# Attention and MoE block on one core: softmax halves by column chunk, merged loads, LoRA pieces between the steps, four expert pairs in whole fp32

## The chip, the cores and the metric

The kernel runs on one core of a Trainium2 chip. The metric is device time in microseconds (us). A core has a matrix engine (TensorE, PE; its weight loads are shown apart as PEld), VectorE (DVE), ScalarE (ACT), GpSimd (POOL), and a sync engine (SP) that here issues most of the transfers from memory. The engines run their own instruction lists in order and meet at semaphores.

## The reference, cut

One layer over 128 tokens (4 batches of 32, width 256), all in fp32: a causal cross-attention, a self-attention whose four projections carry a rank-16 LoRA update, and a mixture of 32 experts with 4 chosen for each token, each behind a layer norm and added to the residual stream.

```
x = x + xattn(layernorm(x), ctx, Wq, Wkv, Wout)          # 16 heads of 16, causal, ctx has 64 columns
x = x + attn(layernorm(x), W + 0.5 * A @ B for q, k, v, o)  # with biases
h = layernorm(x)
s = sqrt(softplus(h @ router.T)); pick top 4 of s + bias; p = s / sum(s)
x = x + sum_e p_e * ffn_e(h) + ffn_shared(h)
ffn(h) = (silu(clip(h @ wg.T)) * clip(h @ wu.T)) @ wd.T  # clip at +-7, inner width 128
```

## The kernel before

All 128 tokens fill the 128 partitions, and nothing is looped but heads, chunks and experts. Width 256 is two chunks c of 128. The residual stream is kept in PSUM twice: `bY` (tokens on partitions) and `bXT` (transposed). The work is one dependent sequence, in three stages.

**Cross-attention** (a = 0). TensorE centres x (L390 to L391), projects keys from the context (L395) and queries (`project_T`, L323), and computes `values` (L332) ahead of `scores` (L344, L348). VectorE spreads the keys over heads (`spread_keys`, L713), takes the row maximum and subtracts it (`shift_half`, L722, L724). ScalarE copies the values into `v_heads` (`copy_v`, L578), then does the exponentials (`exp_half`, L570). TensorE transposes the probabilities (L357) and multiplies them by the values (`attend`, L365); VectorE divides (`normalise_heads`, L752, L754); TensorE transposes (L372), ScalarE copies (L608), and the output projection is added to `bY` (L376) and `bXT` (L380). A half of a softmax is one value of g, that is, of the 64-row group of the keys; each half writes both column chunks. In the original the columns of the output weights are permuted to fit this (`order`).

**Self-attention** (a = 1). The norm takes its statistics from `bY` (L780), GpSimd raises the variance to -0.5 (L282), TensorE spreads it (L441), and VectorE writes the normed `xnT` (L791). Keys, queries, values and the same softmax follow. The projections' weights had the LoRA update merged before: eight small matmuls (`merge_lora` of TensorE, L316, in two blocks of four, two of which run at the same time in different rows of the array) and VectorE's additions (`merge_lora`, L744, and L784 with `wo_mean`, L788). ScalarE's `woc` (L629) is the centred output weight.

**Mixture of experts.** The 32 experts go as 16 pairs. Gate and up weights of a pair (512 KB) are loaded to `gu_raw` (8 buffers). They aren't multiplied as fp32: ScalarE rounds them to fp32r (`gu_high`, L591), GpSimd subtracts to get the rest (`gu_low`, L291, two instructions a pair), the activations are split in the same way (L638, L640, L810), and TensorE makes three products for each of two chunks (`gate_up_half`, L500), six matmuls of 512 columns a pair. TensorE starts on pairs 1 to 5 while VectorE, ScalarE and GpSimd work out the router (L836 to L869: a chain of small operations, some 30 columns wide, each waiting for the one before). Then, for each pair: `clip` (L827), `silu_unit` (L667), `gate_h` (L880), `transpose_h` (L516), `hT_unit` (L672), `down` (L525), with `gate_up(n + 4)` between. GpSimd runs through `gu_low` without regard to the router. `keep_warm` (L309) puts idle-time matmuls of 512 columns at ten places.

The sync queue issues eleven loads (L236), then gate-and-up loads (`load_gu`, L242), of which those from the ninth on wait for `gu_lo_ready` (their buffer), and down loads (`load_dn`, L245). The last step copies `bY` out (L894).

## Time and profile before

| | before |
|---|---|
| time, median of 3 runs (lowest to highest) | 82.14 us (82.06 to 82.21) |
| the profiled execution | 81.89 us |
| its span, first to last instruction | 79.8 us |
| PE, PEld, DVE, ACT, POOL busy | 71.0, 54.8, 46.6, 42.8, 43.5 us |
| mean granted TensorE clock | 0.976 |

The profiled execution stands 0.25 us below the median, and 2.1 us of it lie outside its span. Positions below are microseconds from the start of the span. Busy time of TensorE includes the idle-time matmuls. A matmul on fp32 operands shows as two records, one on fp32r or bf16 operands as one, and a transpose as one.

### The profile page before, as it was taken

What the parts mean: (1) busy time and instruction counts of PE and PEld (TensorE: products, weight loads), DVE (VectorE), ACT (ScalarE), POOL (GpSimd) and SP (SyncE); (2) the same over time, 40 slices, a digit from 0 to 9 for tenths busy, and PEclk for the clock granted to TensorE, in tenths of its full rate; (3) what the DMA queues carried; (4) which work ended last, traced back from release to release, by engine and by line L of the source; (5) the groups of instructions that cost most, each with busy time, mean ns of one, the idle gap of its engine ahead of it and who ended that gap; (6) DMA issues with size and microseconds to landing.
All of it is one profiled execution on the core that took longest, in us unless ns stands there. A gap on an engine that the chain in (4) does not pass through costs nothing.

```text
span 79.8 us, 1534 instructions
## 1 busy us (share of the span) xinstructions
PE 71.0 (89%) x557; PEld 54.8 (69%) x557; DVE 46.6 (58%) x118; ACT 42.8 (54%) x90; POOL 43.5 (54%) x49
## 2 busy tenths in 40 slices
PE   2999999696989999999618999999999999999960
PEld 1388675484966676887306788887888878888840
DVE  2028675377775706999999854566444664449320
ACT  1513951929359288406916986668866633336400
POOL 7200200549999216990830799999999994000000
PEclk9999999999999999999995699999999999999999
DMA  1998999999999999279718209970000000000001
GB/s 27 319 242 237 383 417 402 410 409 412 398 391 405 388 402 390 101 187 306 304 18 273 103 8 267 375 267 3 0 0 0 0 8 0 0 0 0 0 0 66
DMA packets 6440, 15.80 MB, mean 198 GB/s; under 512 B 737, under 2 KB 1634, under 8 KB 6434
## 3 DMA queue, kind: packets, MB, share of 16 engines
q1 hardware_dynamic: 6210, 15.49, 54.5%
q10 hardware_dynamic: 224, 0.23, 1.0%
q8 instruction: 4, 0.07, 0.3%
q14 instruction: 2, 0.02, 0.1%
HBM read 15.59 MB, written 0.13 MB: 197 GB/s over the span
## 4 chain that ended last, share of the span: by engine, by line
PE 57%; DVE 16%; DMA 9%; SPq 6%; issue 3%; ACT 3%; POOL 1%
PE bY L525 17%; DMA gu_raw<-moe_w_dram 9%; SPq L236 6%; PE bB L500 6%; PE bXT L516 5%; PE bC L500 4%; PE bA L500 4%; PE bE L500 4%; PE bD L500 4%; PE bY L376 2%; PE bXT L467 2%; PE bA L332 2%; DVE gu_clip L827 2%; PE bY L550 2%; DVE key L862 1%
## 5 line engine op out<-in xcount | busy, mean ns | idle before, releaser
L291 POOL TENSOR_TENSOR gu_w<-gu_raw,gu_w 128x512 fp32r<-128x512 f32 x32 | 39.9, 1288 | 15.7 <-ACT gu_w L591 15.7
L591 ACT ACTIVATE gu_w<-gu_raw 128x1024 fp32r<-128x1024 f32 x16 | 16.7, 1050 | 1.6 <-DMA gu_raw<-moe_w_dram 1.6
L525 PE MATMUL bY<-dn_w,hT 128*128 128x256 f32 x64 | 16.3, 380 | 0.0
L672 ACT ACTIVATE hT<-bXT 128x256 f32<-128x256 f32 (+1 forms) x17 | 6.4, 377 | 14.4 <-PE bXT L516 14.4
L525 PEld LDWEIGHTS bY<-dn_w,hT 128*128 128x128 f32 x64 | 11.0, 190 | 0.9
L516 PE MATMUL bXT<-first_sb,h 128*128 128x128 f32 x33 | 6.7, 282 | 2.4 <-DVE h L880 2.4
L516 PEld LDWEIGHTS bXT<-first_sb,h 128*128 128x128 f32 x33 | 4.8, 145 | 5.1 <-DVE h L880 2.8
L500 PE MATMUL bB<-gu_w,xnT_parts 128*128 128x512 f32 x24 | 7.9, 461 | 0.1
L500 PEld LDWEIGHTS bB<-gu_w,xnT_parts 128*128 128x128 f32 x24 | 5.0, 218 | 1.5 <-DVE xnT_parts L810 0.5
L282 POOL TENSOR_TENSOR rstd<-var_eps,inv_sqrt_power 128x1 f32<-128x1 f32 x3 | 1.7, 554 | 6.9 <-DVE var_eps L698 5.3
L500 PE MATMUL bC<-gu_w,xnT_parts 128*128 128x512 f32 x18 | 5.3, 428 | 0.0
L500 PE MATMUL bE<-gu_w,xnT_parts 128*128 128x512 f32 x18 | 5.1, 417 | 0.0
L500 PE MATMUL bA<-gu_w,xnT_parts 128*128 128x512 f32 x18 | 5.1, 417 | 0.0
L500 PE MATMUL bD<-gu_w,xnT_parts 128*128 128x512 f32 x18 | 5.1, 416 | 0.0
L309 PE MATMUL bE<-warm_sb 128*128 128x512 bf16 x7 | 3.1, 559 | 1.4 <-DVE warm_sb L759 1.4
L880 DVE SCALAR_TENSOR_TENSOR h<-gu_clip,gate,bB 128x128 f32<-128x128 f32 x8 | 2.4, 345 | 2.6 <-ACT bB L667 2.6
L500 PEld LDWEIGHTS bE<-gu_w,xnT_parts 128*128 128x128 f32 x18 | 3.4, 188 | 0.7
L500 PEld LDWEIGHTS bA<-gu_w,xnT_parts 128*128 128x128 f32 x18 | 3.4, 188 | 0.7
L500 PEld LDWEIGHTS bD<-gu_w,xnT_parts 128*128 128x128 f32 x18 | 3.4, 188 | 0.7
L500 PEld LDWEIGHTS bC<-gu_w,xnT_parts 128*128 128x128 f32 x18 | 3.4, 189 | 0.7
L880 DVE SCALAR_TENSOR_TENSOR h<-gu_clip,gate,bE 128x128 f32<-128x128 f32 x6 | 1.8, 345 | 3.1 <-ACT bE L667 3.1
L880 DVE SCALAR_TENSOR_TENSOR h<-gu_clip,gate,bD 128x128 f32<-128x128 f32 x6 | 1.8, 344 | 2.5 <-ACT bD L667 2.5
(208 smaller groups left out, 130.1 us busy)
## 6 DMA issues: line engine op xcount, KB each, us to landing
gu_raw<-moe_w_dram SPq DMA_DIRECT2D x16, 512.0 KB, 8.3
dn_w<-moe_w_dram SPq DMA_DIRECT2D x16, 256.0 KB, 6.3
aw_sb<-attn_w_dram SPq DMA_DIRECT2D x2, 512.0 KB, 6.5
shared_sb<-shared_w_dram SPq DMA_DIRECT2D x1, 384.0 KB, 10.1
xwq_sb<-x_wq_dram SPq DMA_DIRECT2D x1, 256.0 KB, 3.4
lora_sb<-lora_dram SPq DMA_DIRECT2D x1, 256.0 KB, 4.1
xwo_sb<-x_wo_dram SPq DMA_DIRECT2D x1, 256.0 KB, 6.2
first_sb<-first_dram ACTq DMA_DIRECT2D x1, 130.0 KB, 2.8
```

The lines of the kernel that those rows point to most:

```text
L236: sp.dma_start(dst, src).then_inc(ld[name], 16)
L282: nc.gpsimd.tensor_tensor(rstd[:, n:n + 1], var_eps[:, n:n + 1], inv_sqrt_power[:], ALU.pow).then_inc(rstd_ready, 1)
L291: nc.gpsimd.tensor_tensor(gu_w[:, p % SLOTS, 1, cols], gu_raw[:, p % RAW, cols], gu_w[:, p % SLOTS, 0, cols], ALU.subtract).then_inc(gu_lo ...
L309: nc.tensor.matmul(bank[:, :], warm_sb[:, 0:128], warm_sb[:, :], start=True, stop=True)
L332: last = nc.tensor.matmul(bank[j * S:(j + 1) * S, b * NG * HD:(b + 1) * NG * HD], x_t(k)[:, b * S:(b + 1) * S], w(k).rearrange("p (n j d) ...
L376: return nc.tensor.matmul(bY[:, 0:D], heads_outT[:, a, g, :], w[:, g, :], start=False, stop=(g == DC - 1), skip_group_check=True)
L500: last = nc.tensor.matmul(bGU[n % 5][:, 0:GU], xnT_parts[:, a, k, :], gu_w[:, (n - 1) % SLOTS, w, k * GU:(k + 1) * GU], start=(k == 0 and ...
L516: last = nc.tensor.transpose(bHT[n % 2][:, e * T:(e + 1) * T], h[:, n % 2, e, :], ident)
L525: last = nc.tensor.matmul(bY[:, 0:D], hT[:, n % 2, e, :], dn_w[:, at:at + D], start=False, stop=(n == PAIRS and e == 1), skip_group_check= ...
L591: nc.scalar.activation(gu_w[:, p % SLOTS, 0], gu_raw[:, p % RAW], ACT.Copy).then_inc(gu_hi_ready, 1)
L672: nc.scalar.activation(hT[:, n % 2, 0:width], bHT[n % 2][:, 0:width * T], ACT.Copy).then_inc(hT_ready, 1)
L880: last = nc.vector.scalar_tensor_tensor(h[:, n % 2, e], gu_clip[:, n % 4, e, 1, :], weight_e, bank[:, e * 2 * I:e * 2 * I + I], ALU.mult, ...
```

## The change

What it does, part by part:

1. **Halves by column chunk.** In both softmaxes a half is now one chunk c, with the two row groups g in two banks side by side (`bP[c]`, a tile of two banks). Scores of half c need queries and keys of chunk c alone, and the score matmuls alternate between row groups. Each of the 8 score matmuls of a half now raises `scores_ready`. Output weights need no permuting.
2. **Order of the cross-attention.** The values come behind the scores; their copies are shared between ScalarE (j = 0, 1) and VectorE (j = 2, 3), and the copy of the transposed probabilities as well. The variance of the first norm no longer comes from VectorE's statistics: ScalarE squares the centred x, and two one-column matmuls sum it.
3. **Loads.** x transposed, identity, centring matrix and head mask are one load (`head`, 264 KB), x and the causal mask one (`x_mask`), context and both key and value weights one (`ctx_kv`), the cross-attention's output weights part of `small`. The sync queue issues seven loads before the experts' instead of eleven; ScalarE's queue two, as before.
4. **LoRA pieces.** Each of the eight small matmuls stands alone or in twos at a place where TensorE waits, and VectorE merges them in seven additions. `keep_warm` stays at the start (6) and behind the keys (1). `wo_mean` is ScalarE's.
5. **Four whole pairs.** Pairs 0 to 3 are multiplied as fp32 straight from `gu_raw` (two matmuls of 512 columns, K = 128, a pair). ScalarE and GpSimd convert only pairs 4 to 15. ScalarE does two conversions before the router (pairs 4, 5) where it did six.
6. **GpSimd waits.** Behind pairs 4 and 5 it waits for the third norm and then for `gate_ready`, the end of the router.
7. **Load conditions.** The loads come in the order 4, 5, 6, 0, shared, 1, 2, 3, 7; pairs 8 to 11 wait for `gu_lo_ready` of pairs 4 to 7, pairs 12 to 15 for `gu_ready` of pairs 0 to 3.

The diff, cut to its core:

```diff
@@ constants and tiles
-WARM = dict(start=5, keys=1, heads0=1, headsT0=1, rstd=2, norm=2, probs1=2, attend1=2, heads1=1, headsT1=1)
+WARM = dict(start=6, keys=1)
+WHOLE = 4
+def raw_slot(p):
+    return p if p < RAW else (p - WHOLE) % RAW
@@ sync
+            for name, dst, src in (("head", head_sb[:], head), ("xwq", xwq_sb[:], x_wq), ("lora", lora_sb[:], lora),
+                                   ("aw_kq", aw_sb[:, 0:2], attn_w[:, 0:2]), ("small", small_sb[:], small),
+                                   ("aw_vo", aw_sb[:, 2:4], attn_w[:, 2:4]), ("rows", rows_sb[:], rows)):
             def load_gu(p):
-                if p >= RAW:
+                if p >= RAW + WHOLE:
+                    sp.wait_ge(gu_ready, p - RAW - WHOLE + 2)
+                elif p >= RAW:
                     for c in range(DC):
                         sp.wait_ge(gu_lo_ready[c], p - RAW + 1)
@@ gpsimd
             inverse_sqrt(0)
+            inverse_sqrt(1)
...
-            for p in range(PAIRS):
+            for p in range(WHOLE, PAIRS):
                 for c in range(DC):
-                    if (p, c) == (0, 1):
-                        inverse_sqrt(1)
-                    if (p, c) == (4, 1):
+                    if (p, c) == (WHOLE + 2, 0):
                         inverse_sqrt(2)
+                        pool.wait_ge(gate_ready, 1)
                     gu_low(p, c)
@@ tensor
+            def scores(a, c):
+                for g in range(2):
+                    r = slice(64 * g, 64 * g + 64)
+                    if a == 0:
+                        nc.tensor.matmul(bP[c][:, g, 0:128], causal_sb[:, 0:128], causal_sb[:, 128:],
+                                         start=True, stop=False, skip_group_check=True)
+                for b in range(B):
+                    for g in range(2):
+                        r = slice(64 * g, 64 * g + 64)
+                        nc.tensor.matmul(bP[c][b * S:(b + 1) * S, g, 0:G * S], qT[r, a, c, b * S:(b + 1) * S],
+                                         k_heads[r, c, :, b * S:(b + 1) * S],
+                                         start=(a == 1), stop=True, skip_group_check=True).then_inc(scores_ready, 1)
...
+            for c in range(DC):
+                pe.wait_ge(q_ready, c + 1)
+                pe.wait_ge(k_ready, c + 1)
+                scores(0, c)
+            values(bE, lambda k: ctx_sb[L:2 * L, 0:T], lambda k: ctx_sb[L:2 * L, T:T + D], 1, range(B))
...
+            transpose_probs(0, 1)
+            merge_lora(0, 0)
+            pe.wait_ge(probsT_dve_ready, 1)
+            pe.wait_ge(v_act_ready, 1)
+            pe.wait_ge(v_dve_ready, 1)
             attend(0, 0)
+            merge_lora(0, 1)
+            pe.wait_ge(probsT_act_ready, 1)
             attend(0, 1)
+            merge_lora(1, 0)
+            merge_lora(3, 0)
+            transpose_heads(0, 0)
+            merge_lora(1, 1)
+            merge_lora(2, 0)
+            transpose_heads(0, 1)
...
+            def gate_up_whole(n, k):
+                return nc.tensor.matmul(bGU[n % 5][:, 0:GU], xfT[:, k, :], gu_raw[:, raw_slot(n - 1), k * GU:(k + 1) * GU],
+                                        start=(k == 0), stop=(k == DC - 1))
...
-            for n in range(2, 6):
+            for n in range(2, WHOLE + 1):
                 gate_up(n)
+            pe.wait_ge(xt_lo_ready, 1)
+            gate_up(WHOLE + 1)
             transpose_h(0, width=1)
+            transpose_h(1)
@@ scalar
-            copy_v(range(G), range(B), bV[0]).then_inc(v_act_ready, 1)
-            exp_half(0, 0)
-            exp_half(0, 1)
-            copy_probsT(0)
-            copy_probsT(1)
-            gu_high(0)
+            exp_half(0, 0)
+            copy_v(0, range(B), bE[:, 0:D])
+            exp_half(0, 1)
+            copy_v(1, range(B), bE[:, 0:D]).then_inc(v_act_ready, 1)
+            nc.scalar.activation(probsT[:, 1], bP[1][:, 0, 0:DC * T], ACT.Copy).then_inc(probsT_act_ready, 1)
             for c in range(DC):
                 act.wait_ge(headsT_psum, c + 1)
...
+            gu_high(WHOLE)
...
-            gu_high(2)
-            gu_high(3)
+            gu_high(WHOLE + 1)
...
-            gu_high(5)
...
-            gu_high(6)
             nc.scalar.preload_act_table(ACT.Silu)
+            gu_high(WHOLE + 2)
             silu_unit(0)
             silu_unit(1)
+            gu_high(WHOLE + 3)
@@ vector
             shift_half(0, 0)
             shift_half(0, 1)
+            copy_probsT(0, 0)
+            copy_v(2, range(B), bE[:, 0:D])
+            copy_v(3, range(B), bE[:, 0:D]).then_inc(v_dve_ready, 1)
             dve.wait_ge(ld["aw_kq"], 16)
-            merge_lora(0)
-            merge_lora(1)
+            merge_lora(0, 0)
             normalise_heads(0, 0)
             normalise_heads(0, 1)
+            merge_lora(0, 1)
+            merge_lora_whole(1)
...
-            nc.vector.tensor_scalar(wo_mean[:], wo_sum[:], -1.0 / D, None, ALU.mult).then_inc(wo_mean_ready, 1)
```

## Rows read from the trace of the kernel before

**Rows 1.** The profile's page: busy time by engine; the chain's shares.

```profile
PE 71.0 (89%) x557; PEld 54.8 (69%) x557; DVE 46.6 (58%) x118; ACT 42.8 (54%) x90; POOL 43.5 (54%) x49
...
PE 57%; DVE 16%; DMA 9%; SPq 6%; issue 3%; ACT 3%; POOL 1%
```

**Rows 2.** Windows A:B in us: busy (records) by engine, clock, DMA share, GB/s.

```profile
39.20:41.60 2.40, 0.02 (x2) 0.02 (x1) 2.23 (x10) 0.96 (x3) 1.48 (x2) 1.00 0.13 49
42.40:44.00 1.60, 1.60 (x5) 1.31 (x6) 1.60 (x5) 1.20 (x2) 0.00 (x0) 0.50 0.87 328
```

**Rows 3.** The chain in order of time, experts' stage: start, us, what.

```profile
43.93 2.10 PE bB L500 x6
...
47.11 1.41 PE bC L500 x6
48.52 0.22 PE bXT L516 x2
48.74 0.87 PE bY L525 x4
...
77.27 0.42 DVE y_sb L894
```

**Rows 4.** Timeline of VectorE in the router: start, us, operation.

```profile
32.10 1.30 DVE L836 SCALAR_TENSOR_TENSOR clip_at<-var_eps,rstd 128x1 f32<-128x1 f32 x2 [0.66 <-POOL rstd L282]
...
33.59 1.00 DVE L842 TENSOR_SCALAR den<-one_plus 128x32 f32<-128x32 f32 x1
...
35.01 0.83 DVE L844 TENSOR_TENSOR den<-den,e_abs 128x32 f32<-128x32 f32 x1
...
35.88 0.19 DVE L846 SCALAR_TENSOR_TENSOR ratio<-ln_one_plus,den 128x32 f32<-128x32 f32 x1
...
38.35 1.16 DVE L862 SCALAR_TENSOR_TENSOR key<-score,small_sb 128x32 f32<-128x32 f32 x1
...
40.07 0.67 DVE L866 SCALAR_TENSOR_TENSOR weight<-replaced,score 128x33 f32<-128x33 f32 x1
```

**Rows 5.** Timeline, other engines around the router.

```profile
31.45 0.53 PE L536 MATMUL bXT<-small_sb,xfT 128*128 128x32 f32 x4
...
38.11 1.28 ACT L660 ACT_TABLE_LOAD   x1
...
44.34 16.22 POOL L291 TENSOR_TENSOR gu_w<-gu_raw,gu_w 128x512 fp32r<-128x512 f32 x13 [3.65 <-ACT gu_w L591]
```

**Rows 6.** Timeline of the two attentions, steps that mark the stages.

```profile
7.01 0.65 PE L332 MATMUL bE<-wv_sb,ctx_sb 64*32 64x64 f32 x32
...
8.52 0.42 DVE L722 TENSOR_REDUCE row_max<-bA 128x8 f32<-128x256 f32 x1 [0.73 <-PE bA L348]
...
9.17 0.48 PE L316 MATMUL bD<-lora_sb 16*128 16x256 f32 x1
...
9.17 0.48 PE L316 MATMUL bC<-lora_sb 16*128 16x256 f32 x1
...
12.25 0.21 DVE L752 RECIPROCAL inv_sum<-bE 128x8 f32<-128x8 f32 x1 [0.52 <-PE bE L365]
...
13.83 1.06 ACT L591 ACTIVATE gu_w<-gu_raw 128x1024 fp32r<-128x1024 f32 x1 [1.60 <-DMA gu_raw<-moe_w_dram]
...
16.34 0.43 DVE L780 BATCH_NORM_STATS2 stats<-bY 128x6 f32<-128x256 f32 x1 [1.71 <-PE bY L376]
...
17.89 1.18 DVE L788 TENSOR_SCALAR wo_mean<-wo_sum 128x2 f32<-128x2 f32 x1
...
18.98 0.41 DVE L791 TENSOR_TENSOR xnT<-xcT,bA 128x256 f32<-128x256 f32 x1
```

**Rows 7.** Timeline, VectorE's step that ends the attentions.

```profile
30.10 0.29 DVE L814 COPY xfT<-bXT 128x128 f32<-128x128 f32 x1 [2.36 <-PE bXT L380]
```

**Rows 8.** The chain in order of time, one of its idle-time matmul pairs.

```profile
25.24 0.43 PE bB L309 x2
```

**Rows 9.** The view of the tile gu_raw: issue to landing of its 16 loads.

```profile
DMA to landing us min/median/max: 3.7/8.3/13.3
```

More of the change, by code:

```diff
@@ L178, in build @@
         q_ready = sem("q_ready")
[L179 removed]
+        lora_psum = [sem(f"lora_psum_{m}") for m in "kqvo"]
         lora_merged = sem("lora_merged")
@@ L509, in gate_up @@
                 for k in range(DC):
-                    last = gate_up_half(n, k)
+                    if n <= WHOLE:
+                        pe.wait_ge(ld_gu[n - 1], 16)
+                        last = gate_up_whole(n, k)
+                    else:
+                        pe.wait_ge(gu_lo_ready[k], n - WHOLE)
+                        for a, w in HI_LO:
+                            last = nc.tensor.matmul(bGU[n % 5][:, 0:GU], xnT_parts[:, a, k, :],
+                                                    gu_w[:, (n - 1) % SLOTS, w, k * GU:(k + 1) * GU],
+                                                    start=(k == 0 and a == w == 0), stop=(k == DC - 1 and a == 1))
                 last.then_inc(gu_ready, 1)
@@ new lines @@
+    head[:, XT:XT + DC * T] = x.T.reshape(DC, 128, T).transpose(1, 0, 2).reshape(128, -1)
+    head[:, IDENT:IDENT + 128] = np.eye(128, dtype=np.float32)
+    head[:, CENTRE:CENTRE + 128] = np.eye(128, dtype=np.float32) - np.float32(1.0 / D)
+    head[:, HMASK:HMASK + G] = np.arange(128)[:, None] // HD % G == np.arange(G)[None, :]
+    causal = np.zeros((128, 128 + G * S), np.float32)
+    causal[:, 0:128] = np.eye(128)
+    hidden = np.arange(S)[None, :] > (np.arange(T) % S)[:, None]
+    causal[:, 128:] = np.tile(np.where(hidden, -1e30, 0.0), (1, G))
@@ L950 @@
     moe = np.concatenate([gu, dn], axis=2).reshape(128, -1)
-    arrays = {"x": x, "x_t": x.T.reshape(DC, 128, T).transpose(1, 0, 2), "first": first, "small": small,
-              "causal": causal, "ctx_k": ctx_k, "w_v": w_kv[D:].T,
-              "x_wq": chunked(v["L0_xattn_Wq"]), "x_wo": chunked(v["L0_xattn_Wout"][:, order]), "lora": lora,
-              "rows": rows, "attn_w": attn_w, "shared_w": shared, "moe_w": moe}
+    arrays = {"head": head, "x_mask": x_mask, "small": small, "ctx_kv": ctx_kv, "x_wq": chunked(v["L0_xattn_Wq"]),
+              "lora": lora, "rows": rows, "attn_w": attn_w, "shared_w": shared, "moe_w": moe}
     arrays = {n: np.ascontiguousarray(a) for n, a in arrays.items()}
```

556 lines of the change are left out of this document (252 added, 304 removed).

## The prediction

> **What bounds the kernel now.** I read the page's busy times and the chain's shares first [rows 1]: TensorE is busy 89% of the span but carries 57% of the chain, so for a good part of the time somebody else decides. The chain in order of time then shows three stages. From 46 us to the end it is TensorE alone, with a period of 1.41 + 0.22 + 0.87 = 2.50 us a pair [rows 3]. From 30 to 42 us it is the router on VectorE [rows 4]; TensorE has pairs 1 to 5 to do meanwhile, runs out at 39.2 and stands 2.4 us, after which its granted clock falls to half [rows 2]. The first product behind takes 2.10 us where it otherwise takes 1.41 [rows 3]. Before 30 us the chain changes engines at every step, and I followed it by the steps that mark the stages [rows 6, 7].
>
> **Start of the span to the statistics of the first residual (16.34, [rows 6]).** The row maximum of half one starts at 8.52. In front of the scores the values (0.65) go away; I count the context's load, issued 0.4 earlier, as 0.25 for keys and queries; two one-column products for the variance come in, four records behind the queries, at the price of the logits' four (0.45 by their spacing, [rows 5]); eight score products alternate between row groups, where two products at once in two row groups are seen for LoRA (both at 9.17, [rows 6]), minus 0.35. Sum -0.65 - 0.25 + 0.45 - 0.35 = -0.8, so 7.7. From there to the first reciprocal I keep the 3.7 us (12.25 becomes 11.4): the values' copies are now behind the scores, but shared between two engines. From the reciprocal to the statistics it took 4.1 us. In it ScalarE waited for a load until 13.83 and converted to 14.89 before it could copy the heads [rows 6]. That conversion is now behind the copies. New sum from 11.4: first division 0.5, second half attended and divided to 12.6, one LoRA couple ahead of each heads' transpose (0.43 each, a 256-column product alone being 0.87/2, [rows 3]) to 13.1, copy to 13.5, two products to 14.2. That is 2.8 instead of 4.1, and -2.1 in all.
>
> **To the normed x (18.98).** VectorE had `wo_mean` in front of it: 1.18 us for two numbers a partition, while GpSimd was converting [rows 6]. It moves to ScalarE; of its 1.18 us some 0.7 lay beside the wait for GpSimd's power and the spreading product, so it frees 0.5 to 0.9. Against it LoRA piece (3, 1), 0.43, stands ahead of that spreading product, about 0.3 of it on the path. Net -0.5: xnT at 16.4, in all -2.6.
>
> **To the end of the attentions (30.10, [rows 7]).** 11.1 us before. The chain holds idle-time matmuls twice 0.43 and once 0.22 [rows 8]; they go. Scores of half one wait for chunk 0 only, a gain of some 0.4. What comes in: `woc` (two ScalarE steps) and a values' copy now stand ahead of the exponentials (I take +0.2), a LoRA merge ahead of the row maximum (0.42, +0.3), the values' second half between the two transposes (0.65, in place of the fillers there). Net -1.05: xfT at 26.45, in all -3.65. LoRA in six places takes 2.6 us of TensorE where two blocks took 1.7; except for the 0.3 and the couples above, it lies in waits. If none did, it would cost 6 x 0.43 = 2.6; if all, I gain 0.7 more.
>
> **The router and the first pairs.** Taking positions as before (all less 3.65 at the end): TensorE starts on the whole pairs at 30.5. A whole pair is two fp32 products of 512 columns; 256 columns cost 0.43, so 1.73 a pair against 1.41 [rows 3]: dearer by 0.32. Its work is 4 x 1.73 + 1.41 (pair five) + 0.45 (logits) + 0.87 (shared) = 9.6, to 40.1. The router's small steps with both inputs in SBUF took 1.30 (for two), 1.00, 0.83, 1.16 and 0.67 where GpSimd had an instruction running, and 0.19 for the same width at 35.88 where it had none [rows 4]. With GpSimd waiting I take 0.4, 0.2, 0.2, 0.2, 0.25: -3.7, of which 0.7 is lost because `den` waits for ScalarE's sum. So `gate`, ready at 41.3, comes at 38.3. ScalarE has the table load (1.28, [rows 5]), one conversion (1.06, [rows 6]) and two silus ahead of the first gated pair: h(1) at 39.3. TensorE is still at work until 40.1, a cover of 0.8 us: its idle 2.4 us and the slow clock go together. Transposes, a wait of 0.3 for hT and the shared down product end at 41.2; the next pair at full clock at 42.6, where it ended at 46.03. So -3.4 here.
>
> **The rest** keeps 2.50 us a pair if conversions keep up. GpSimd made 13 in 16.22 us, 2.50 a pair [rows 5]: exactly TensorE's pace, so what lead it has at the start it keeps. It begins pair 6 at 38.3, done 40.8, wanted at 43.7 + 0.7: a lead of 3.6. The load of pair 10 now waits on the sync queue for `gu_low` of pair 6, and pairs 11 to 15 and their down loads are queued behind it. Issued at 40.8 it lands 3.7 to 13.3 later, median 8.3 with the engines full [rows 9]. The queue is empty at that point, so I take 3.7: 44.5, wanted by ScalarE at 45.0. The first loads come in fewer, wider pieces; the very first, 264 KB, may land 0.3 earlier or 0.5 later than two of half the size did.
>
> **Sum.** 79.8 - 3.65 - 3.4 = 72.75 us of span, + 2.1 outside = 74.85 against the profiled 81.89; the median of the runs stands 0.25 above that execution: **75.1 us**.
>
> Each of 8 score products now raises a semaphore. The Trainium skill ("TensorE: Matmul & The Clock Gate", The cost: per-tile semaphore tail) fits 26.3 ns for each further increment. By that rule, as an estimate, a half ends 0.18 us later, four halves at most 0.7, and the sum would be 75.3 to 75.8. No row of this trace shows such a row of increments.
>
> **The rivals.**
> (a) *The clock falls in the attentions*, since the idle-time matmuls go. For: the clock did fall after TensorE stood [rows 2]. Against: that was 2.4 us, and the longest gap in my new order is some 0.6. Price as at the router: 2.10 - 1.41, and about 1.0 on the products just ahead, 1.7: 76.8. Chance 0.14.
> (b) *Conversions or their loads set the pace.* For: equal pace, and pair 10's load is held until 40.8. If it lands after 8.3, ScalarE stands 4.1 us with hT behind it; slack there is 1.3: +2.8, 77.9. Against: empty queue. Chance 0.1.
> (c) *The router's stalls aren't GpSimd's.* Then h(1) stays near 42, TensorE stands 2 us and the clock falls: only about 1.1 of the 3.4 stays, 77.4. Against: the 0.19 row. Chance 0.04.
> (d) *Slower than before: the clock stays low from the attentions into the pairs.* Without fillers TensorE enters the experts' stage at half clock, whose 9.6 us of products then double: 75.1 + 9.6 = 84.7. It decides from 7 us of products done at half clock on the path. For: before, the products behind the stand ran at half clock although they were packed [rows 2]. Against: from 47.11 on they are at full speed again, some 5 us after the stand [rows 3], and my order has no such stand. Chance 0.03.
> (e) *The first stages don't shrink as summed*: waits that I took for hidden are on the path, half of 3.65 is gone, 76.9. Chance 0.12. The forecast itself, 73.7 to 76.5, keeps 0.57.
>
> **How the numbers follow.** The lower end takes all covers as full: LoRA hidden (0.7) and 0.8 more for `wo_mean` and the load, 73.6. The upper end takes in (a), (c), (e) and most of (b): 77.9. About 0.2% is what a measurement of this kernel tells from no change; all cases but (d) are faster by more: 0.96 faster, 0.01 the same, 0.03 slower.
>
> **What would show it.** Router steps of 0.2 us with GpSimd idle; no gap of TensorE between the pairs and the first transpose, and a granted clock of 1.0 from 40 us on; xnT near 16.4 and xfT near 26.5; first output statistics near 14.2; a period of 2.50 to the end; GpSimd's last conversion some 3 us before it is wanted. Wrong would be: a gap of TensorE before the heads' transposes, ScalarE waiting for `gu_raw` of pair 10, a clock under 1.0 between 5 and 30.

## The result, and the profile after

| | before | after |
|---|---|---|
| median (lowest to highest), same chip | 82.17 us (82.06 to 84.07) | 79.49 us (79.29 to 80.41) |
| ratio after/before, 95% interval | | 0.970 (0.960 to 0.980) |
| profiled execution, its span | 81.89, 79.8 us | 79.66, 77.9 us |

Ratios rest on the executions that agree with each other; where too few did, only the times are given. The change makes the kernel faster by 2.7 us where I had forecast 7.0, outside my range. The page of the changed kernel, busy times and shares of the chain, against [rows 1]:

```profile
PE 72.9 (94%) x544; PEld 53.4 (69%) x544; DVE 42.7 (55%) x119; ACT 38.0 (49%) x84; POOL 33.7 (43%) x42
...
PE 85%; DMA 5%; ACT 3%; DVE 3%; issue 1%
```

VectorE's 16% of the chain are 3% now. TensorE carries 85% of it, 57% before: that is the first sign of what I missed, since in that kernel little that TensorE does is free.

**The router and the pairs.** The timeline of VectorE after, against [rows 4], and GpSimd's first six conversions behind the router, against [rows 5]:

```profile
33.56 0.23 DVE L848 SCALAR_TENSOR_TENSOR clip_at<-var_eps,rstd 128x1 f32<-128x1 f32 x2 [0.44 <-POOL rstd L293]
...
34.47 0.18 DVE L854 TENSOR_SCALAR den<-one_plus 128x32 f32<-128x32 f32 x1 [0.34 <-ACT one_plus L669]
...
35.07 0.19 DVE L856 TENSOR_TENSOR den<-den,e_abs 128x32 f32<-128x32 f32 x1
...
37.76 0.19 DVE L874 SCALAR_TENSOR_TENSOR key<-score,small_sb 128x32 f32<-128x32 f32 x1
...
38.51 0.20 DVE L878 SCALAR_TENSOR_TENSOR weight<-replaced,score 128x33 f32<-128x33 f32 x1
...
38.95 0.30 DVE L881 TENSOR_SCALAR gate<-weight,weight_sum,rstd 128x32 f32<-128x32 f32 x1
...
39.33 7.51 POOL L304 TENSOR_TENSOR gu_w<-gu_raw,gu_w 128x512 fp32r<-128x512 f32 x6 [5.80 <-DVE gate L881]
```

Each step that took 0.67 to 1.30 us takes 0.18 to 0.23. `gate` is ready 7.8 us after xfT, where it took 11.2. Two windows of the changed kernel (columns as in [rows 2]), and the chain behind them (against [rows 3]):

```profile
36.00:40.00 4.00, 4.00 (x11) 1.77 (x10) 3.60 (x17) 3.71 (x7) 0.67 (x1) 1.00 0.01 2
40.00:44.00 4.00, 3.85 (x19) 2.93 (x18) 3.13 (x8) 2.93 (x7) 4.00 (x4) 1.00 0.27 51
```

```profile
42.67 1.40 PE bP L529 x6
44.08 0.22 PE bXT L537 x2
44.29 0.87 PE bY L546 x4
```

The stand of 2.4 us and the fall of the clock to half are gone, and the period is 2.50 as before.

**The front.** The marks of the stages on VectorE after, against [rows 6] and [rows 7]:

```profile
10.65 0.43 DVE L737 TENSOR_REDUCE row_max<-bP 128x8 f32<-128x256 f32 x1 [0.61 <-PE bP L362]
...
14.57 0.21 DVE L771 RECIPROCAL inv_sum<-bP 128x8 f32<-128x8 f32 x1
...
18.39 0.43 DVE L801 BATCH_NORM_STATS2 stats<-bY 128x6 f32<-128x256 f32 x1 [0.64 <-PE bY L387]
20.96 0.42 DVE L808 TENSOR_TENSOR xnT<-xcT,bP 128x256 f32<-128x256 f32 x1 [1.03 <-PE bP L460]
...
31.49 0.29 DVE L827 COPY xfT<-bXT 128x128 f32<-128x128 f32 x1 [2.41 <-PE bXT L391]
```

The first row maximum came 2.13 us later than before, not 0.8 earlier, and xfT 1.39 later, not 3.65 earlier. The chain of waits from the start, after:

```profile
0.73 3.66 DMA head_sb<-head_dram
...
4.43 0.80 PE bP L400 x2
...
6.51 1.15 PE bP L405 x4
...
8.20 1.31 PE bP L334 x8
```

The merged first load lands 3.66 us after its issue, and TensorE starts at 4.43 where it had started at 3.55. And the products behind it are slow: keys (L405) 1.15 us, queries (L334) 1.31. The experiments show what they are at full speed.

### The profile page after: what moved, and what is told of

Read it like the earlier page. It is cut to its first block, busy times and chain, and to the rows that moved or that the text cites. A ratio compares the mean times of both kernels' runs of the same rounds, so it can differ in the third digit from the quotient of the medians.

```text
span 77.9 us, 1484 instructions
## 1 busy us (share of the span) xinstructions
PE 72.9 (94%) x544; PEld 53.4 (69%) x544; DVE 42.7 (55%) x119; ACT 38.0 (49%) x84; POOL 33.7 (43%) x42
## 4 chain that ended last, share of the span: by engine, by line
PE 85%; DMA 5%; ACT 3%; DVE 3%; issue 1%
PE bP L529 18%; PE bY L546 18%; PE bP L515 7%; DMA head_sb<-head_dram 5%; PE bXT L537 4%; PE bP L334 4%; PE bE L529 4%; PE bXT L391 3%; PE bY L387 2%; PE bE L328 2%; PE bE L515 2%; PE bP L376 2%; PE bP L362 2%; PE bXT L328 2%; PE bP L400 2%; PE bP L405 1%
## 5 line engine op out<-in xcount | busy, mean ns | idle before, releaser
L304 POOL TENSOR_TENSOR gu_w<-gu_raw,gu_w 128x512 fp32r<-128x512 f32 x24 | 29.9, 1282 | 5.8 <-DVE gate L881 5.8
L529 PE MATMUL bP<-gu_w,xnT_parts 128*128 128x512 f32 x60 | 17.8, 432 | 0.0
L546 PE MATMUL bY<-dn_w,hT 128*128 128x256 f32 x64 | 16.3, 380 | 0.0
L892 DVE SCALAR_TENSOR_TENSOR h<-gu_clip,gate,bP 128x128 f32<-128x128 f32 x26 | 7.9, 345 | 10.2 <-ACT bP L685 10.1
L606 ACT ACTIVATE gu_w<-gu_raw 128x1024 fp32r<-128x1024 f32 x12 | 12.6, 1053 | 1.4 <-DMA gu_raw<-moe_w_dram 1.4
L529 PEld LDWEIGHTS bP<-gu_w,xnT_parts 128*128 128x128 f32 x60 | 11.3, 189 | 2.8 <-issue 0.5
L839 DVE TENSOR_SCALAR gu_clip<-bP,clip_at 128x512 f32<-128x512 f32 x13 | 10.4, 806 | 0.0
L537 PE MATMUL bXT<-head_sb,h 128*128 128x128 f32 x33 | 6.2, 271 | 0.0
L685 ACT ACTIVATE bP<-gu_clip,rstd 128x256 f32<-128x256 f32 x13 | 6.1, 471 | 0.0
L537 PEld LDWEIGHTS bXT<-head_sb,h 128*128 128x128 f32 x33 | 4.6, 140 | 2.1
L515 PE MATMUL bP<-gu_raw,xfT 128*128 128x512 f32 x12 | 5.8, 602 | 0.0
```

The costliest lines, as they stand in the source:

```text
L304: nc.gpsimd.tensor_tensor(gu_w[:, p % SLOTS, 1, cols], gu_raw[:, raw_slot(p), cols], gu_w[:, p % SLOTS, 0, cols], ALU.subtract).then_inc(g ...
L515: return nc.tensor.matmul(bGU[n % 5][:, 0:GU], xfT[:, k, :], gu_raw[:, raw_slot(n - 1), k * GU:(k + 1) * GU], start=(k == 0), stop=(k == D ...
L529: last = nc.tensor.matmul(bGU[n % 5][:, 0:GU], xnT_parts[:, a, k, :], gu_w[:, (n - 1) % SLOTS, w, k * GU:(k + 1) * GU], start=(k == 0 and ...
L537: last = nc.tensor.transpose(bHT[n % 2][:, e * T:(e + 1) * T], h[:, n % 2, e, :], ident)
L546: last = nc.tensor.matmul(bY[:, 0:D], hT[:, n % 2, e, :], dn_w[:, at:at + D], start=False, stop=(n == PAIRS and e == 1), skip_group_check= ...
L606: nc.scalar.activation(gu_w[:, p % SLOTS, 0], gu_raw[:, raw_slot(p)], ACT.Copy).then_inc(gu_hi_ready, 1)
```

## The experiments

**The head's load and the start.** Two edits, each alone on the changed kernel. The first splits the head load:

```diff
 # sync queue
-("head", head_sb[:], head)
+("head", head_sb[:, 0:DC * T], head[:, 0:DC * T])
 # ScalarE's queue, first
+act.dma_start(head_sb[:, DC * T:], head[:, DC * T:]).then_inc(ld["head"], 16)
...
 # tensor and vector
-wait_ge(ld["head"], 16)
+wait_ge(ld["head"], 32)
```

> The changed kernel with one thing undone: the first 258 KB come again as two loads at the same moment, 128 KB of x transposed from the sync queue and 130 KB of matrices from ScalarE's. Theory S (start): the merged head landed at 4.43 where the two halves landed by 3.55 in the kernel before; TensorE had run out of start matmuls at 3.72, stood 0.7 us, and then ran its next products at half speed (0.21 us apart for 128 columns, not 0.11) until about 8. Then here the first product starts near 3.6, the products are at full speed from about 4.3, the row maximum starts near 9.0 and not 10.65, and the time falls by 1.5 to 1.8 us, to about 77.8. Rival O (order): the stage is long because of its new order (variance products, shared copies), the load only moves its start: the row maximum comes 0.9 earlier at most, time 78.6. Rival N: other waits fill the gap, no change, 79.5.

The second adds two start matmuls:

```diff
-WARM = dict(start=6, keys=1)
+WARM = dict(start=8, keys=1)
```

> The changed kernel with eight start matmuls in place of six, so that TensorE has no stand before the head lands at 4.43. Theory S: it is the stand of 0.7 us that kept the clock low. Then the products from 4.5 on run at full speed (0.11 us apart) from about 4.5 on, the row maximum starts near 9.6, time about 78.5. Rival: the clock rises at its own moment whatever TensorE does before, and nothing but the landing matters: products still 0.21 us apart until about 8, time 79.5 or 79.6.

Split, both halves landed 2.6 to 2.9 us after issue, the first product started at 3.67, the first row maximum at 8.29: 2.36 earlier. The time was 78.92 us (78.48 to 80.95), ratio to before 0.961 (0.953 to 0.969). The marks are those of theory S, the time isn't, for a reason that stands below. With eight start matmuls it was 78.58 us (78.20 to 80.05), ratio 0.959 (0.950 to 0.968), near the 78.5 of theory S: TensorE had no stand, its first product started at 4.37, its products were at full spacing from 6.1 on, and the row maximum came at 9.18. The split head's chain from the start to the queries:

```profile
3.73 0.74 PE bP L400 x2
...
5.30 0.64 PE bP L405 x4
...
6.26 0.89 PE bP L334 x8
```

The same four records of the keys take 0.64 us here and 1.15 in the changed kernel. There are two losses, not one: 0.76 us for the later load, and 1.6 us because TensorE rose to full speed late. The columns of the granted clock do not show it: here one window, first of the changed kernel, then of the one that splits the head and shifts LoRA (below), where the clock rose as early as in this one:

```profile
5.40:7.40 2.00, 2.00 (x10) 1.74 (x8) 0.35 (x2) 0.90 (x3) 0.00 (x0) 1.00 0.95 233
```

```profile
5.40:7.40 2.00, 2.00 (x19) 1.82 (x17) 1.40 (x3) 0.86 (x3) 0.00 (x0) 1.00 0.92 243
```

Both say 1.00 and busy 2.00, but 10 records passed in one and 19 in the other. Near the start it is the spacing of the products that tells the clock. Whether the rise is early isn't set by the load alone. Five kernels have the merged head and six start matmuls, and in each TensorE stood 0.5 to 0.7 us ahead of the first product: one rose by 4.6 us (the LoRA-free one below, row maximum at 8.52), the changed kernel and three others only after 7.6 (10.65 to 10.74). Of the five with the split head, four were at full spacing by 4.7 us and one at 6.4. And the rise moves where nothing was changed: the run b2_convert_later below has the instructions of the kernel before up to 30.6 us, yet its products were slow until 6.6, and its row maximum came at 9.37, not 8.52:

```profile
9.37 0.42 DVE L722 TENSOR_REDUCE row_max<-bA 128x8 f32<-128x256 f32 x1 [1.04 <-PE bA L348]
```

The Trainium skill ("TensorE: Matmul & The Clock Gate", What's actually happening) says that the number of slow products at the start varies between runs; the traces agree, with 0.85 us between these two and 2.2 us between the extremes of the merged head. The same place puts the loss under 1% of a typical span; here it is 1.6 of 77.9 us, 2%.

But the rest of the split head's front was worse: in its trace the granted clock fell behind the heads' transposes, from 14.9 to 18.3 us. Windows around it:

```profile
15.00:16.00 1.00, 1.00 (x4) 0.60 (x3) 0.40 (x1) 1.00 (x2) 0.00 (x0) 0.50 1.02 402
...
17.00:18.00 1.00, 1.00 (x6) 1.00 (x6) 0.93 (x6) 0.00 (x0) 0.50 (x1) 0.50 1.01 402
```

That is rival (a). The output projection took 1.60 + 1.71 us on the chain, 1.06 + 0.89 in the changed kernel: 1.4 us lost, and what the early start had won was mostly given back.

**Merging the head alone, in the kernel before.** Identity, centring matrix and mask come with x transposed in one load, and ScalarE's queue issues one load less:

```diff
-xT_sb = sb("xT_sb", [128, DC, T])
-first_sb = sb("first_sb", [128, FIRST])
+head_sb = sb("head_sb", [128, DC * T + FIRST])
...
-act.dma_start(first_sb[:], first).then_inc(ld["first"], 16)
```

> The kernel before with one thing of the change done alone: x transposed (128 KB) and the first matrices (130 KB) come as one load of 258 KB from the sync queue, where two came at the same moment from two queues. Theory S: the load lands near 4.2 and not 3.55, 0.6 to 0.9 later, TensorE stands behind its start matmuls, which here end at 3.6, and if its clock then stays low the products up to the queries run at half speed: time 82.14 + 0.8 to + 2.2, so 82.9 to 84.3. Rival: the kernel before has slack there, since x, context and query weights are awaited too (first keys at 5.16, first scores at 7.6): 82.1 to 82.3.

It landed 3.0 us after issue; first product at 3.74 (before 3.55), row maximum at 9.07 (8.52), span 80.3. The times ran from 82.38 to 85.36 us, median 84.28. So the merge puts off the first product by 0.2 us in the kernel before (and by 0.76 in the changed one, 4.43 against 3.67). The rest of the 0.55 at the row maximum goes with a later rise of the clock, which moved by more in b2_convert_later with nothing changed there; that the 0.5 of span is the merge's isn't shown. It gains nothing in either kernel.

**GpSimd's wait.** The wait for `gate_ready` goes; the order and all else stay:

```diff
 inverse_sqrt(2)
-pool.wait_ge(gate_ready, 1)
```

> The changed kernel without GpSimd's wait for the end of the router: it goes on with pair 6 as soon as ScalarE has rounded it. ScalarE rounds pair 6 only behind the router's last step, so GpSimd may have nothing to do before. Theory P (wait is what frees VectorE): small router steps with two inputs in SBUF are stretched to 0.7 to 1.2 us again, gate comes 2 to 3 us later than 39.25, TensorE stands 1 to 2 us, time 81 to 82. Rival Q (moving ScalarE's conversions behind the router has already emptied GpSimd): router steps behind the table load at most are touched, gate within 0.5 us of 39.25, covered by TensorE, time 79.5.

Without the wait the time was 79.36 us, ratio to before 0.961 (0.951 to 0.971): no worse than with it. GpSimd stood all the same, as its timeline shows, since its next conversion needs ScalarE's, and that stands behind the table load:

```profile
41.84 1.37 DVE L880 TENSOR_SCALAR gate<-weight,weight_sum,rstd 128x32 f32<-128x32 f32 x1
41.89 8.73 POOL L304 TENSOR_TENSOR gu_w<-gu_raw,gu_w 128x512 fp32r<-128x512 f32 x7 [5.49 <-ACT gu_w L605]
```

It waits 5.49 us for ScalarE where it had waited 5.80 for `gate`. One step of the router alone, `gate`, now meets it: 1.37 us where it was 0.30. The step behind it came later by that, but TensorE was at work until 44.4 all the same: from xfT to the end of gate_up(6) it is 12.58 us with the wait and without. So my mechanism was right (no GpSimd instruction beside the router, short steps; one beside it, a long step), but the line of the change that does it is ScalarE's order, not GpSimd's wait. The Trainium skill ("SBUF — State Buffer", Who interferes with whom) says that a VectorE instruction with two SBUF inputs contends with a GpSimd instruction that reads SBUF, and `key`, with two, took 1.16 us beside one and 0.19 without. It lists `tensor_scalar`, the kind of `gate`, among those that can take the shared ports too; 1.37 us against 0.30 agrees.

**The same order in the kernel before.** ScalarE's conversion of pair 5 moves from ahead of the router's activations to behind them (where pair 6 stood), that of pair 6 behind the first two silus; nothing else:

```diff
-            gu_high(5)
...
-            gu_high(6)
+            gu_high(5)
             nc.scalar.preload_act_table(ACT.Silu)
...
+            gu_high(6)
```

> The kernel before with ScalarE's conversions of pairs 5 and 6 moved behind the router's last step and behind the first two silus; nothing else. GpSimd then has nothing to convert between about 33.3 (pair 4 done) and the end of the router. Theory P (GpSimd's instructions stretch the router, and their feed is ScalarE's order): den, key and weight take 0.2 us each where they took 0.7 to 1.2, gate is ready near 38.7 and not 41.3, TensorE's stand of 2.4 us shrinks below 0.5 and its clock stays; against it pair 6 is converted late (GpSimd begins it near 38.5, TensorE wants it near 40), at a cost of some 0.5 us. Time 79.0 to 80.0. Rival: GpSimd's pace of 2.50 us a pair is TensorE's, so its late start is carried to the end as waits for gu_lo of 1 to 2 us: time 80.5 to 81.5. Rival Q: no change of the router, 82.1.

79.93 us (79.65 to 81.13), ratio 0.978 (0.969 to 0.987): 2.2 us by the medians, 1.8 by the ratio, from two moved calls. The timeline of it, router steps and TensorE's first transpose:

```profile
33.92 0.18 DVE L842 TENSOR_SCALAR den<-one_plus 128x32 f32<-128x32 f32 x1
...
37.51 1.17 DVE L862 SCALAR_TENSOR_TENSOR key<-score,small_sb 128x32 f32<-128x32 f32 x1
...
39.24 0.69 DVE L866 SCALAR_TENSOR_TENSOR weight<-replaced,score 128x33 f32<-128x33 f32 x1
...
40.78 0.33 PE L516 MATMUL bXT<-first_sb,h 128*128 128x128 f32 x1 [1.23 <-DVE h L880]
```

`den` is short, with no conversion beside it; `key` and `weight` are long, beside the one that GpSimd starts at 37.33. `gate` is ready 10.0 us after xfT (11.2 before, 7.8 in the changed kernel), later than I expected, and TensorE stands 1.23 us, not under 0.5, where it had stood 2.38. Its clock stays at 1.00, and on the chain the next product behind takes 1.40 us instead of 2.10 [rows 3]. From xfT to the end of that product it is 13.35 us, against 15.9 before and 12.6 in the changed kernel: 2.6 of the 3.35. Most of what the change brings around the router needs no whole pairs.

**LoRA left out.** All eight small products and VectorE's additions of them are gone, so the update is missing from the self-attention's weights; the two that are kept, for o, add zero times another tile. The core of the edit:

```diff
-            merge_lora(0, 0)
...
             attend(0, 0)
-            merge_lora(0, 1)
...
             attend(0, 1)
-            merge_lora(1, 0)
-            merge_lora(3, 0)
             transpose_heads(0, 0)
-            merge_lora(1, 1)
-            merge_lora(2, 0)
             transpose_heads(0, 1)
...
```

> The changed kernel with the LoRA update left out: none of the eight small matmuls, no merge of the weights of q, k and v, and for o two VectorE operations of the same size that add nothing. Its result lacks the LoRA term. Theory L (TensorE is the bound between 12 and 21 us and the pieces cost what they take, 0.62 alone and 0.63 for a couple): from the first reciprocal to xnT 2.5 us or more go (6.4 becomes 3.9), some 0.3 more behind, time 76.5 to 77. My forecast's view (they lie in waits but for about 1.2 us): 78.3. Rival V (VectorE's merges are the cost, not the matmuls): the same fall in time, but TensorE would show gaps now where the pieces stood; the trace tells the two apart by who waits at the heads' transposes.

First reciprocal to statistics took 2.51 us (3.82 with LoRA), statistics to xnT 2.12 (2.57), xnT to xfT 10.60 (10.53). LoRA costs 1.31 + 0.45 = 1.76 us on the path, all of it before xnT; from the first row maximum to xfT it is 1.61, since two other steps came out 0.08 and 0.07 longer. The times ran from 75.94 to 80.48 us, median 77.58; 2.13 us of the distance to the changed kernel's trace is the early rise and the earlier first product, not LoRA. Rival V (VectorE's merges) fails: with LoRA no wait stands at the heads' transposes and TensorE is busy throughout, without it TensorE waits there 0.48 us for VectorE's division. The chain of the changed kernel shows where it sits:

```profile
13.42 0.62 PE bXT L328 x2
...
14.52 0.62 PE bXT L328 x2
...
15.51 0.41 PE bE L328
...
16.14 0.26 PE bP L383
...
19.81 0.62 PE bP L328 x2
...
28.46 0.62 PE bY L499 x2
```

A single piece takes 0.62 us, not 0.43. A couple, one piece in each of two row groups, takes 0.63: from 15.51 to 16.14, and again from 16.40 to 17.03. So the second piece of a couple costs 0.01 us, and singles are the dear form. A product of 256 columns with all 128 rows takes 0.43 on the same chain (L428, at 12.56), and the one that adds the bias, with a single row (L499), 0.62 like LoRA's with 16. So part of the 0.62 isn't columns. TensorE's weight loads, changed kernel:

```profile
16.07 0.14 PEld L383 LDWEIGHTS bP<-head_sb,heads_out 128*128 128x128 f32 x1 [0.33 <-issue]
```

A load of all 128 rows behind a product that uses 16 of them stands 0.33 us first, and no semaphore is named for it. That it waits for the small product to leave the array is my reading; TensorE's own records have no gap there, and no run tests it.

**LoRA in couples.** Pieces (3, 0) and (1, 0) join the two that stood alone before the attended halves, and (3, 1) joins (2, 1) behind the spreading of the power:

```diff
             merge_lora(0, 0)
+            merge_lora(3, 0)
...
             merge_lora(0, 1)
+            merge_lora(1, 0)
...
-            merge_lora(1, 0)
-            merge_lora(3, 0)
...
-            merge_lora(3, 1)
...
             merge_lora(2, 1)
+            merge_lora(3, 1)
```

> The changed kernel with its eight LoRA products in four couples in place of two singles, two couples and two singles: (0,0) with (3,0), (0,1) with (1,0), (1,1) with (2,0), and (2,1) with (3,1), the last behind the product that spreads the norm and not ahead of it. A couple took 0.63 us where a single took 0.62. Theory L (TensorE is the bound from 13 to 21 us, each piece costs what it takes): two pieces fewer on the path, first reciprocal to xnT 6.4 becomes 5.2, time 78.3. Rival (pieces lie in waits): same as the changed kernel, 79.5. Rival V: VectorE's merges come later behind the heads and the gain is under 0.5.

78.03 us (77.09 to 78.72), ratio 0.951 (0.922 to 0.981). Reciprocal to xnT took 3.21 + 2.12 = 5.33 us, 1.06 less than the 6.39 of the changed kernel, with all of VectorE's merges in place: theory L. Its row maximum was late, at 10.74, as there.

**One increment for each row group.** Only the last score product of each row group raises the semaphore, two in place of eight a half:

```diff
-    start=(a == 1), stop=True, skip_group_check=True).then_inc(scores_ready, 1)
+    start=(a == 1), stop=True, skip_group_check=True)
+if b == B - 1:
+    last.then_inc(scores_ready, 1)
...
-dve.wait_ge(scores_ready, 8 * (2 * a + c + 1))
+dve.wait_ge(scores_ready, 2 * (2 * a + c + 1))
```

> The changed kernel with two raises of scores_ready for each half of a softmax (the last product of each row group) where there were eight. By the increments' price as a page states it, six fewer would end each half 0.16 us earlier, 0.3 to 0.6 us in all: time 78.9 to 79.2. By my sum, which gave them nothing: 79.5. The trace shows it in the stretch from the last score product to the row maximum, 0.35 us in the changed kernel.

The times say nothing: 78.34 to 86.73 us at mean clocks from 0.918 to 1.0. The traces say something. In the second attention the scores of half one start at 23.50 and the row maximum at 24.23 in the changed kernel, 0.73 us; with two increments at 26.45 and 27.03:

```profile
26.45 0.56 PE bP L362 x16
27.03 0.43 DVE row_max L739
```

That is 0.58, so 0.15 less. In the first attention the row maximum starts 0.29 us behind the end of the products in the changed kernel (10.36, 10.65), and 0.13 here (10.60, 10.73): 0.16 less. The rule that I had weighed (the Trainium skill, "TensorE: Matmul & The Clock Gate", The cost: per-tile semaphore tail) makes six increments fewer worth 6 x 26.3 ns = 0.158 us, as an estimate, and the trace agrees with it at both places. It acts once an attention: half two of the row maximum stands behind VectorE's own work (11.45 after 11.11, changed kernel). So it costs 0.3 us of the sum, inside the 0.2 to 0.7 that I had set beside it.

**Idle-time matmuls put back.** With the head split, two of them stand again ahead of the heads' transposes; and, further down, three with the couples:

```diff
-WARM = dict(start=6, keys=1)
+WARM = dict(start=6, keys=1, heads0=1, headsT0=1)
```

> The changed kernel with the head split again into two loads, as in the run a1_split_head, and with two idle-time matmuls of 512 columns put back between the heads' steps of the cross-attention. In a1_split_head the granted clock was 0.50 from 14.9 to 18.2 in the profiled execution, and its mean was 0.975 to 0.978 in three of four. Theory C (the clock falls there for want of wide products): clock 1.0 in every execution, 1.6 us less than a1_split_head minus 0.5 for the two fillers on the path: 77.6 to 77.9. Rival (the fall hangs on something else, as the moment at which the clock rose at the start): clock near 0.976 again, time 79.2 to 79.4.

78.05 to 87.13 us, median 79.79, ratio 0.963 (0.946 to 0.981). In its trace the clock stood at 0.50 from 14.3 to 21.1 us all the same, and the mean clock was 0.956 and 0.957 in two of six executions, 1.0 in the others. An idle-time matmul does not keep the clock up by being there.

**Split head and couples together**, both edits as above:

> The changed kernel with the split head of a1_split_head and the four LoRA couples of a6_lora_couples together. The two act on different stretches, so the intervals add: first product near 3.7, first reciprocal to xnT 5.3, xnT to xfT 10.5. Executions in which the clock rises before the first products and doesn't fall behind the heads: 8.3 + 3.9 + 5.3 + 10.5, xfT at 28.1, time 76.1. Executions in which it falls from 14.9 to 18.2 as in a1_split_head: 1.5 more, 77.5. Rival: the couples' gain needs the stands that the late head gave, sum below the parts, 77.5 without a fall.

76.98 us (76.22 to 83.65, six executions), ratio 0.939 (0.931 to 0.947); profiled 76.22, span 74.4. It beats both kernels, and the two gains add: xfT was expected at 28.1 and the time at 76.1 us without a fall. Its marks on VectorE:

```profile
8.28 0.42 DVE L738 TENSOR_REDUCE row_max<-bP 128x8 f32<-128x256 f32 x1 [0.71 <-PE bP L362]
...
15.40 0.43 DVE L802 BATCH_NORM_STATS2 stats<-bY 128x6 f32<-128x256 f32 x1 [0.64 <-PE bY L387]
...
28.05 0.29 DVE L828 COPY xfT<-bXT 128x128 f32<-128x128 f32 x1 [2.40 <-PE bXT L391]
```

The clock stayed up in all six, also in the one of 83.65 us, which no trace explains. The same with three idle-time matmuls (before the first probabilities' transpose, and at the two places above):

> a8_split_couples with three idle-time matmuls of 512 columns between its steps: ahead of the second transpose of the probabilities, behind the first heads' product and behind the first heads' transpose. Each costs at most 0.25 us on TensorE. Theory C (wide products there keep the clock up): clock 1.0 in all or nearly all executions, time 76.5 to 76.9, less spread than a8_split_couples. Rival: falls as often as without them, median 0.6 above a8_split_couples.

77.69 us (76.59 to 85.83, six), ratio 0.944 (0.934 to 0.953). No fall in six either, and no gain: from the row maximum to the statistics it is 7.67 us against 7.12, so the three cost 0.55 us of path, and they aren't shown to help.

**The first variance on VectorE.** On top of split head and couples, ScalarE's squares and the two one-column products are replaced by the old statistics:

```diff
-nc.scalar.activation(xsq[:, 0], xcT[:, 0, 0], ACT.Square).then_inc(sq_ready, 1)
...
-last = nc.tensor.matmul(bY[:, 511:512], xsq[:, k, :], minus_mean[:, 0:1], ...)
...
+nc.vector.bn_stats(stats[:, 0], x_sb).then_inc(sq_ready, 1)
+nc.vector.bn_aggr(moments[:, 0], stats[:, 0]).then_inc(minus_var_psum, 1)
```

> a8_split_couples with the first norm's variance on VectorE again (two statistics instructions on x and one scalar step, 0.42 + 0.18 + 0.15 us behind the keys' spreading) in place of two squares on ScalarE and two one-column products. Theory T (TensorE sets this stretch): the row maximum starts 0.35 earlier, 0.3 us off the time. Rival V: VectorE ends the keys near 6.9, then needs 0.8 more for the variance, and the row maximum waits for it at 7.8 at most, which is before the scores; GpSimd's power comes 0.3 later and the exponential waits: no gain.

Inconclusive. Three of seven executions took 75.94 to 76.94 us, as low as the LoRA-free kernel's best; their ratio to before, 0.936 (0.923 to 0.950), is that of the kernel without this edit, 0.939. In the other four the mean clock was 0.91 to 0.98, up to 83.75 us, and the median of all was 79.24. In the profiled one the load of x, which the split head puts third in ScalarE's queue, landed 7.7 us after its issue (4.3 in a1_split_head, 5.0 to 6.0 in the other three with a split head). TensorE, for the mask in the same load, stood 1.68 us, and VectorE as long:

```profile
9.34 0.43 DVE L776 BATCH_NORM_STATS2 stats<-x_mask_sb 128x6 f32<-128x256 f32 x1 [1.69 <-DMA x_mask_sb<-x_mask_dram]
```

At the end of that stand the granted clock fell, and it stayed at 0.50 from 9.4 to 23.0 us. What the squares cost was not to be read beside that.

## Why the prediction was wrong, step by step

| step (us) | before | predicted | after | split head, couples |
|---|---|---|---|---|
| start to first row maximum | 8.52 | 7.7 | 10.65 | 8.28 |
| to first reciprocal | 3.73 | 3.7 | 3.92 | 3.92 |
| to statistics | 4.09 | 2.8 | 3.82 | 3.20 |
| to xnT | 2.64 | 2.2 | 2.57 | 2.12 |
| to xfT | 11.12 | 10.05 | 10.53 | 10.53 |
| xfT to `gate` ready | 11.2 | 8.2 | 7.8 | 7.8 |
| xfT to end of gate_up(6) | 15.9 | 12.5 | 12.6 | 12.6 |
| from there to the end | 33.8 | 33.8 | 33.8 | 33.8 |

The profiled execution is 4.81 us above my sum of 74.85: 5.04 from the first five rows, 0.11 from the pairs, and -0.34 because 1.76 us and not 2.1 lie outside the span. Everything missed is in the front.

**Start, missed by 2.95.** I gave the first load "0.3 earlier or 0.5 later" for the range and zero in the sum. It was 0.88 later (4.43 against 3.55). The late rise of the clock costs 1.62: first product to row maximum takes 6.22 us in the changed kernel and 4.60 in the one with split head and couples, same instructions. I had no rival for it; rivals (a) and (d) looked for a clock that falls, not for one that hasn't risen. The remaining 0.45 is the sum itself (4.60 against 7.7 - 3.55 = 4.15). In it, alternating row groups was to give 0.35. By the timelines the score products of a half take 0.45 us where they took 0.64, so 0.19 came of it. But the row maximum starts 0.29 us behind their end where it was 0.07, and 0.16 of that goes with six of the seven further increments: from the first score product to the row maximum it is 0.74 us against 0.71, no gain.

**Reciprocal to statistics, missed by 1.02.** The term "one LoRA couple ahead of each heads' transpose, 0.43 each" failed. The sum has 0.5 us for it, from 12.6 to 13.1; by the run without LoRA the pieces cost 1.31 here. A couple takes 0.63, and piece (0, 1), which I had in a wait, stands on the chain for 0.62. That is 0.8 of the 1.02. The other 0.2 is the sum without LoRA, which comes to 2.3 where the run took 2.51. I took an edit in a wait for free from a kernel in which ScalarE was late here; the same change took that wait away, and TensorE was what came last next. Windows that end 0.3 to 0.4 us ahead of the statistics, before and then after:

```profile
14.00:16.00 2.00, 1.35 (x8) 0.91 (x7) 0.63 (x1) 2.00 (x4) 1.03 (x1) 1.00 1.02 406
```

```profile
16.00:17.00 1.00, 1.00 (x8) 0.47 (x7) 0.45 (x2) 0.28 (x1) 0.00 (x0) 1.00 1.02 397
17.00:18.00 1.00, 1.00 (x7) 0.64 (x6) 0.69 (x1) 0.67 (x2) 0.00 (x0) 1.00 1.06 424
```

ScalarE was busy 2.00 of 2 us and TensorE 1.35; now ScalarE is busy 0.95 and TensorE 2.00. Even so not every piece on the chain is paid in full: those of this stretch take 0.62 + 0.63 + 0.63 = 1.88 us there, and leaving them out returned 1.31.

**To xnT, missed by 0.37**, again LoRA's: piece (3, 1) was to cost 0.3 and costs 0.45 of path by the run without LoRA. The rest, 0.22, is `wo_mean`'s: without the piece the stretch takes 2.12 us, 0.52 less than before, the lower end of my 0.5 to 0.9, where the net of -0.5 had taken 0.8.

**To xfT, missed by 0.48.** I took 1.08 us for idle-time matmuls that stood on the chain. Split at the second attention's row maximum, the stretch was 3.80 + 7.32 before and is 3.27 + 7.26 after. That row maximum in the timeline before, and the chain after from it on:

```profile
22.78 0.42 DVE L722 TENSOR_REDUCE row_max<-bB 128x8 f32<-128x256 f32 x1 [0.27 <-PE bE L348]
```

```profile
24.23 0.44 DVE row_max L737
...
27.23 0.28 ACT v_heads L598
...
27.60 0.86 PE bP L376 x32
```

Ahead of the row maximum the gain is 0.53, more than the 0.4 less 0.3 that I had. Behind it, where all 1.08 us of the removed ones had stood, 0.06 came of it. The chain there now goes through ScalarE: both exponentials and four copies of the values, from 26.38 to 27.51, end just ahead of the first attended product, which starts 3.37 us behind the row maximum where it had started 3.54 behind. I had given ScalarE's steps 0.2. The idle-time matmuls had stood beside work that takes as long, so their time on the chain isn't what their removal returns. No run removes them alone.

**Router and pairs, right**: -3.35 against -3.4. `gate` came 0.4 earlier than summed, TensorE was idle 0.15 us in the two windows from 36 to 44, and the period stayed 2.50. The whole pairs' products, in the timeline of TensorE:

```profile
34.79 3.60 PE L515 MATMUL bP<-gu_raw,xfT 128*128 128x512 f32 x8
```

Eight records are four products, two pairs: 3.60 us with the end of the last, where I had 2 x 1.73. But the reason named first, GpSimd waiting for `gate`, is worth nothing that the run without it shows; ScalarE's later conversions keep GpSimd idle until the router's last step.

**The rivals.** (a), at 0.14, does occur: in the changed kernel one execution of four had a mean clock of 0.957 (80.41 us), of the split head's three of four 0.975 to 0.978. Its price is 1.4 us in the split head's trace against my 1.7. In three other variants the fall is twice as long (6.8 us against 3.4), and in the two of them that keep the changed kernel's work there, the first reciprocal to xnT takes 2.8 to 2.9 us more than the changed kernel's 6.39. It does not explain the profiled execution after, whose clock is 1.00 throughout the attentions. (b) was right in its premise (ScalarE waits for `gu_raw` three times, 1.4 us in total, the longest 0.9) and had no price: the lead covered it. (c) and (d) did not occur. (e), at 0.12, was the case, larger than I had priced it: the front didn't lose half of 3.65 but all of it, and 1.4 more. With an early rise, a split head and LoRA as it is, the front would end at 29.1 (28.05 + 1.06): even then it would have gained 1.0 and not 3.65. The 0.2% that I gave as what a measurement tells from no change was too fine: the kernel before ran from 82.06 to 84.07 us, and the intervals of the ratios are 1% to either side.

**What stays open.** What decides whether the clock falls in the attentions. In the traces of four variants (split head; no wait of GpSimd; two increments; split head with fillers) TensorE was busy 97 to 100% of the microseconds ahead of the fall; so a gap just ahead of it isn't needed, and the gaps that I had looked for in rival (a) are not its only sign. In that of the last kernel it came at the end of a stand of 1.68 us and was the longest, 13.6 us. Of the kernel before, no trace shows a fall in the attentions, but two of twelve later executions had mean clocks of 0.938 and 0.958 and have no trace, so that it came with the change isn't shown. Nor does the stand of 2.4 us always bring the fall at the router: four executions of the kernel before had a mean clock of 1.0 and took 80.69 to 81.34 us, and against those the change gains 1.2 to 1.9 us. Six executions without a fall, for split head and couples, are few; that the couples prevent it isn't shown. Nor is it shown what makes the rise early or late: four of five with the split head were early and four of five with a stand ahead of a merged one late, but one of each was not.

## What to carry to other kernels

Before you put work "into a wait", ask whose wait it is and whether the same change ends it: once the late engine is no longer late, every filler is on the path, at its true price with what follows it. A transfer that all else waits for should stay small and split over queues, with an eye on what then stands behind it (here the load of x, 1.68 us late in one trace), and a saved issue isn't a saved microsecond. Look for the cheapest form of a gain first: two conversions moved behind the router brought 1.8 to 2.2 us in the old kernel, most of what the large change measured (2.7 by the medians).

## What the runs showed of the hardware that I had not expected

- The rise of TensorE to full speed at the start moves by 3 us between kernels with the same first instructions (full spacing from 4.6 us, or only after 7.6), costs up to 1.6 us, and doesn't show in the granted clock, which says 1.00 in both.
- The granted clock fell to 0.50 for 3.4 us (14.9 to 18.3) or 6.8 (14.3 to 21.1, 16.1 to 22.9, 16.3 to 23.1) while TensorE had been busy 97 to 100% just ahead, with LoRA pieces of 16 rows, attended heads and transposes; and for 13.6 (9.4 to 23.0) at the end of a stand of 1.68.
- Two LoRA pieces of 16 rows in two row groups take 0.63 us, one alone 0.62, a product of one row and 256 columns 0.62, of 128 rows 0.43; a full-height weight load behind a LoRA piece starts after 0.33 us idle.
- 258 KB in one load landed 3.66, 3.6, 3.4 and (in the kernel before) 3.0 us after issue; in two loads on two queues 2.5 to 3.0. The third load of ScalarE's queue, 192 KB, then landed 4.3 to 7.7 us after its issue.
- Eight increments on a half's score products put off the reader by 0.15 to 0.16 us against two.
